# A transformer block on one core: the list of shared items and the work ahead of the first slot are placed anew

## The reference

```python
xn = _layernorm(x)                                   # x: (8, 512, 256)
Q, K, V = xn @ W_q.T, xn @ W_k.T, xn @ W_v.T         # 16 heads of 16
scores = einsum('bhqd,bhkd->bhqk', rope(Q), rope(K)) * 16 ** -0.5
heads  = einsum('bhqk,bhkd->bhqd', softmax(causal(scores)), V)
attn   = heads.reshape(b, t, d) @ W_o.T
ffn    = fake_quant_fp8(xn) @ fake_quant_fp8(weight).T + bias
return x + attn + ffn
```

## Time and profile before

| | us |
|---|---|
| median of the three runs | 439.68 |
| time of the profiled execution | 439.77 |
| its span (first to last instruction) | 438.0 |
| PE, DVE, ACT, POOL busy, share of the span | 88%, 81%, 66%, 56% |
| the chain that ended last, share by engine | PE 63%, ACT 16%, DVE 10%, issue 7%, POOL 2%, DMA 1% |

### The profile page before, as it was taken

One profiled execution on the slowest core, in us unless ns is written; L12 is line 12 of the kernel. 1 busy time (PEld: TensorE's weight loads), 2 busy tenths in 40 slices (PEclk: granted clock), 3 DMA queues, 4 the chain that ended last, 5 costly groups with the idle time before them and its releaser, 6 DMA issues.

```text
span 438.0 us, 9484 instructions
## 1 busy us (share of the span) xinstructions
PE 384.9 (88%) x2990; PEld 205.9 (47%) x2990; DVE 355.3 (81%) x1380; ACT 290.6 (66%) x487; POOL 245.4 (56%) x266
## 2 busy tenths in 40 slices
PE   7998987878879988998899898989899998898886
PEld 7685543333434544454445444545445433353335
DVE  3899679999888988898888979887989797879104
ACT  3529538567765777587866776676677677669751
POOL 5444263365559548556666666676666565245750
PEclk9996979999989999999999999999999999999999
DMA  8944032302503143302630262018031613020111
GB/s 280 307 146 71 1 94 79 73 2 97 123 0 75 52 157 62 75 27 94 148 75 1 98 171 61 15 52 216 15 62 49 183 38 74 2 99 4 49 49 49
DMA packets 27810, 36.40 MB, mean 83 GB/s; under 512 B 3984, under 2 KB 25872, under 8 KB 26320
## 3 DMA queue, kind: packets, MB, share of 16 engines
q1 hardware_dynamic: 27760, 35.79, 30.2%
HBM read 22.94 MB, written 12.58 MB: 81 GB/s over the span
## 4 chain that ended last, share of the span: by engine, by line
PE 63%; ACT 16%; DVE 10%; issue 7%; POOL 2%; DMA 1%; ACTq 0%; POOLq 0%; SPq 0%; DVEq 0%
PE o_ps L1047 15%; ACT prob L803 12%; PE st_ps L943 9%; PE m_ps L927 9%; PE m_ps L1005 7%; PE m_ps L982 7%; PE s_ps L962 5%; DVE scratch L657 4%; PE m_ps L989 2%; PE s_ps L899 2%; DVE prod L605 2%; DMA q_st<-shift 1%; PE m_ps L1013 1%; DVE prod L604 1%; DVE amax L593 1%
## 5 line engine op out<-in xcount | busy, mean ns | idle before, releaser
L803 ACT ACTIVATE prob<-st_ps,exp_scale 128x512 f32<-128x512 f32 x320 | 202.9, 689 | 98.9 <-PE st_ps L943 98.2
L657 DVE CUSTOM_DVE_ANT_0 scratch<-s_ps,causal 128x512 bf16<-128x512 f32 (+3 forms) x512 | 221.3, 484 | 35.8 <-PE s_ps L962 33.8
L510 POOL TENSOR_SCALAR_AFFINE_SELECT prob<-prob 128x512 f32<-128x512 f32 (+1 forms) x160 | 90.1, 565 | 147.4 <-ACT prob L803 147.3
L943 PE MATMUL st_ps<-q_st,k_st 50*128 50x128 f16 (+3 forms) x512 | 108.9, 303 | 35.4 <-ACT prob L803 26.9
L962 PE MATMUL s_ps<-k_st,q_st 48*128 48x512 f16 (+3 forms) x512 | 109.7, 306 | 4.7 <-DVE rowmax L657 4.4
L943 PEld LDWEIGHTS st_ps<-q_st,k_st 50*128 50x128 f16 x512 | 35.2, 94 | 121.1 <-ACT prob L803 74.6
L1047 PE MATMUL o_ps<-prob,v_sb 128*17 128x512 f32 (+3 forms) x1024 | 82.8, 441 | 1.7 <-POOL prob L510 0.9
L962 PEld LDWEIGHTS s_ps<-k_st,q_st 48*128 48x128 f16 x512 | 34.5, 95 | 15.9 <-DVE rowmax L657 9.0
L657 DVE DVE_READ_ACCUMULATOR2_ANT rowmax<- 128x1 f32 x512 | 41.1, 80 | 0.0
L1047 PEld LDWEIGHTS o_ps<-prob,v_sb 128*17 128x17 f32 x1024 | 23.2, 97 | 30.0 <-issue 23.0
L982 PE MATMUL m_ps<-wv_sb,xnT 128*128 128x256 f32 x128 | 33.7, 408 | 1.5 <-ACT v_sb L810 1.3
(11 more groups left out here) (130 smaller groups left out, 493.5 us busy)
## 6 DMA issues: line engine op xcount, KB each, us to landing
qk_parts<-parts SPq DMA_DIRECT2D x14, 512.0 KB, 3.6
xnT<-x_dram SPq DMA_DIRECT2D x8, 512.0 KB, 8.5
q_st<-qk_parts SPq DMA_DIRECT2D x15, 256.0 KB, 4.2
k_st<-qk_parts SPq DMA_DIRECT2D x15, 256.0 KB, 4.6
x_res<-x_dram SPq DMA_DIRECT2D x7, 512.0 KB, 3.4
out_dram<-x_res SPq DMA_DIRECT2D x7, 512.0 KB, 3.0
...
```

The costliest lines, as they stand in the source:

```text
L510: eng.affine_select(out=ap, in_=ap, compare_op=ALU.is_ge, fill=0.0, base=0, pattern=pat, channel_multiplier=-1).then_inc(masked, 1)
L657: eng.tensor_tensor_reduce(scratch[:, at % 3, col:col + w], s_ps[at % 3][:, col:col + w], causal[:, T - w:T], 1.0, NEG, ALU.add, ALU.max, ...
L803: eng.activation(prob[u][:, half * T:(half + 1) * T], st_ps[ST_BANK[2 * s + half]][:, :], ACT.Exp, scale=exp_scale[:, 0:1]).then_inc(exp_d ...
L943: mm = eng.matmul(st_ps[ST_BANK[i]][:, col:col + T - kb * P], k_rows(n, h, ROWS + SHIFT, slice(kb * P, (kb + 1) * P)), q_rows(n, h, ROWS + ...
```

## The change

The tables are written anew. A batch's 20 shared items become 18, since `at` now turns two blocks of queries into one bank, and ACT copies them in one instruction. Four buffers are doubled: `v_sb`, `x_res` and `xq` have one half per parity of the batch, `attnT` has a place for each of the four blocks. Offsets of a batch's items, before and now:

| item | before | now |
|---|---|---|
| v | 0, 2 | -1, 0 |
| mt | -4, 1, 7, 12 | -4, 1, 6, 11 |
| o | 23, 24, 25, 26 | 23, 24, 27, 28 |
| at | 28, 29, 32, 34 | 27, 33 |
| fin | 31, 34, 36, 38 | 29, 34, 42, 45 |
| qk | -32, -30, -27, -25 | -30, -28, -25, -23 |

Batch 1's projections move from slots -7 to -4 to slots -11, -11, -9 and -8 (a slot -11 is added, with no scores in it). `statistics(4, 5)` moves from ahead of the first slot to slot -9 and `statistics(6, 7)` from -9 to -7; `turn_rows` of 2 to 7 moves from -10, -9, -8, -7, -5, -3 to -10, -8, -6, -5, -3, -2; `normalise` has a table of its own. Two stretches of dummy matmuls (16 and 10) with a wait on DMA between them become one of 24.

```diff
-TURN_SLOT = {2: -LEAD, 3: -LEAD + 1, 4: -LEAD + 2, 5: -LEAD + 3, 6: -LEAD + 5, 7: -LEAD + 7}
+STAT_SLOT, INVERT_SLOT = {4: -9, 6: -7}, {4: -8, 6: -6}
+NORMAL_SLOT = {4: -8, 5: -7, 6: -5, 7: -4}
+TURN_SLOT = {2: -10, 3: -8, 4: -6, 5: -5, 6: -3, 7: -2}
...
-CHAIN = {("rotate", 0): -29, ("high", 0): -28, ("low", 0): -26, ("write", 0): -25, ("rotate", 1): -24, ("high", 1): -23,
-         ("low", 1): -21, ("write", 1): -20, ("read", 0, 0): -19, ("read", 0, 1): -16, ("read", 1, 0): -12,
+CHAIN = {("rotate", 0): -27, ("high", 0): -26, ("low", 0): -24, ("write", 0): -22, ("rotate", 1): -22, ("high", 1): -21,
+         ("low", 1): -19, ("write", 1): -17, ("read", 0, 0): -16, ("read", 0, 1): -14, ("read", 1, 0): -8,
...
-    first, last, loop = (24, 25, 26, 27, 28), (6, 7, 11, 12, 14), (16, 17, 21, 22, 24)
+    first, last, loop = (24, 25, 26, 27, 28), (6, 7, 11, 12, 14), (16, 18, 20, 23, 25)
...
-                n = batch_at(slot, -34, 2)
+                n = batch_at(slot, -32, 2)
                 if n is not None:
                     split_x(n)
...
-                n = residual_at(slot, 29, 17)
+                n = residual_at(slot, 27, 17)
...
-                n = batch_at(slot, -35, 2)
+                n = batch_at(slot, -34, 2)
                 if n is not None:
                     high_x(n)
...
                     copy_turned(n)
-                    if n + 2 < NB:
-                        normalise(n + 2)
+                for n in [n for n, at_slot in NORMAL_SLOT.items() if at_slot == slot]:
+                    normalise(n)
...
+            def turn_two(n, i, bank):
+                turn_attn(n, 2 * i, bank, 0)
+                return turn_attn(n, 2 * i + 1, bank, D)
...
             keep_busy(20)
             eng.wait_ge(low_done[1], 2)
-            keep_busy(16)
-            eng.wait_ge(parts_out[1], 16)
-            keep_busy(10)
+            keep_busy(24)
```

135 lines of the change are left out of this document (64 added, 71 removed).

## The result

The changed kernel takes **447.48 us** (median; 446.93 to 448.82 over 4 runs) against 440.38 us for the kernel before in the same call (439.63 to 443.5): ratio 1.0152, 95% interval 1.0095 to 1.0209. It is slower by 1.5%, where 428.5 us was forecast, 2.5% faster.

A forecast was written before the change was run, and what follows sets the result against it. PE nearly full in steady batches (42.17 of 46.2 us), DVE in batch 0. Gains of 7.2 (batches 2 to 5), 1.9 (batch 1), 0.8 (batch 6) and 1.3 (head) sum to 11.2 us: 428.5 us, range 419.0 to 439.0.

The forecast's parts named there:

- Steady batches: Batches 2 to 5: PE's idle time falls from 4.1 to 2.3 us a period; gain 1.8 each, 7.2 us together.
- Wait (1): Slot 28: PE's V product waits for ACT's copy of heads; 1.0 us a batch, bounds 0.6 and 1.3.
- Wait (2): Slots 14 and 19: ACT's `high` waits behind POOL's 2.5 us rotation; 0.7 us for both, bounds 0 and 1.5.
- Wait (3): Slots 3 to 8: POOL's quantisation, bias, split end just in time for slot 10's projection; 0.2 us, bounds 0 and 2.36.
- Batch 1: Batch 1: the steady 1.8 us plus half of 1.3 for half-clock V products, less 0.6 in slot 19; gain 1.9 us.
- scale of two elements: Batch 1's chain on DVE: 2.07 us beside a POOL operation, kept; with a 1.28 us rotation there, batch gain 2.7.
- Batches 6 and 7: Batch 6 gains 0.8 us, its projection slots staying empty; batch 7 wins a little, loses by `qv`, counted at nothing.
- Head: Start to slot 1: slot 1 at 64 to 65 us; gain 1.3 us, bounds -2 and +4.7.
- the fourth rival: Head: PE at 1.2 GHz up to slot 1 costs 3.3 us more, time 431.8; chance 0.1 within the forecast's 0.5.
- Batch 0 at nothing: Batch 0: DVE sets the pace and its work is the same; gain nothing, bounds -1 and +1.
- POOL's queue: Slot 10 of each batch: PE waits 2.36 us for POOL's late `split_x`; time 444.7, chance 0.08.
- The clock: Head: gaps between PE's turns bring half clock up to slot 1, 3.3 us more, time 431.8; chance 0.1.

The follow-up runs named there:

- e10: Changed kernel with the edits of e5, e2, e7 and e8 together, and the last two turns of heads one slot earlier: 435.19 us, ratio 0.9876.
- e12: The kernel of e10 with ACT's `high` copies one slot later and POOL's split of x moved ahead of the bias: 423.88 us, ratio 0.9595.
- e5: Changed kernel with POOL's two quantisation steps of batch 0 in slots 29 and 30, batch 0's first output product in 32: 442.41 us, ratio 0.9994.
- e2: Changed kernel with ACT's three scalings of the weights in slot 20 behind the copy of V's first half: 445.35 us, ratio 1.0117.
- e4: Changed kernel with batch 6's output products back in slots 151, 154, 156 and 158, its store in 159: 445.83 us, ratio 1.0128.
- e8: Changed kernel with ACT's norms of batches 6 and 7 one slot earlier, in slots -6 and -5: 445.65 us, ratio 1.0070.
- e3: Changed kernel with the head of the kernel before put back: 444.15 us, ratio 1.0092.
- e6: Changed kernel with idle PE products added (6, 6, 6 and 16) in slots 156 to 159: 451.14 us, ratio 1.0197.
- e7: Changed kernel with batch 7's bias on POOL in slot 156 in place of 157: 444.76 us, ratio 1.0055.

## Why the prediction was wrong

- **Steady batches: right.** Forecast 44.4, measured 44.23; 7.7 us for 7.2. The terms were less good than their sum, and that their errors cancelled is luck. PE's work fell by 0.6 us that I had not counted; its idle time is 2.6 us for the 2.3 forecast. Wait (1), the copy of heads, is in the trace with 0.73 us of PE, but was not worth its 1.0: in e10 and e12 it is gone and the period is no shorter. Wait (2), `high` behind the rotation, was costed at 0.7 and was 1.5 (bound 1.5). Wait (3), POOL in slots 3 to 8, was costed at 0.2 and showed nothing, but had only 0.2 us of reserve, which the earlier heads used up.
- **Batch 1: wrong in sign,** 10.3 us longer for 1.9 shorter. Two steps failed. I took POOL's slots of a steady batch for all batches and did not lay batch 0's own row of the table (24 to 28) beside the moved bias, split and product; e5 gives 6.0 us back. And I priced the V item in slot 19 against DVE but did not ask what the one in slot 20 waits for: its bank, freed by a copy that ACT's program has behind three scalings; e2 gives 3.5 back. The half clock on slot 26's V products, which I had hoped to halve, stayed (2.67 us for 2.76), and more was added in slots 20, 29 and 30: 0.89 over the batch for 0.97, where I had named 1.00 from batch 1 on as a sign of being right. The chain's scale of two elements, carried over at 2.07 us, took 0.17: POOL ran nothing beside it, so the rotation that I had put there did not stand there either.
- **Batches 6 and 7: undersized,** 4.5 us gained for 0.8. Batch 7's 2.0 us come from a row of the change that neither the table of the change nor the prediction has: batch 6's output products stand in slots 149, 150, 154 and 155, where they stood in 151, 154, 156 and 158. e4 puts them back and the 2.0 us are gone. Where batch 6's 2.5 come from no run asked.
- **Head: wrong in sign,** slot 1 at 69.3 for 64 to 65. The chain that I summed (norm 6, `high`, norm 7, copies, turn, V) is the one in the trace, but started at 54.6 where my sum had 52.0, and ran at half clock, as the fourth rival had it. The start, 2.6 us late, and what the half clock added behind it (V 3.44 us for 1.99, a turn 1.09 for 0.66) make most of the 4.8. The norm of 6 stood behind the copy of batch 5's turn, which I had ending at 52.0 us; the turn ended at 53.6 and its copy at 54.7. I named the chain and left this order as it was: e8 shows that the norm was free from 51.7 on.
- **Batch 0 at nothing: wrong,** 2.0 us, in e3 still 1.7. DVE was busy 0.57 us more and idle 2.04 for 0.64. Of the idle time 0.73 us are its wait for the spread product behind V, which I had costed at 0.6 and booked to batch 1, though it falls in slot 19; 0.81 are a wait for PE's scores at 82.7 us, in a stretch at half clock that the kernel before does not have there (the granted clock over the batch is 0.84 for 0.95). Why DVE was busier, and why other executions of the same slots took up to 45.4 us, is open.
- **Tail at nothing: wrong,** 4.0 us. The prediction had no step for it. Moving batch 6's products forward out of slots 156 to 158 left PE light in front of the tail, and the clock fell (e4, e6); the bias in front of the last masks kept it low for longer (e7). Batch 7 gained by the same move: undoing it brings 1.5 us net (e4).
- **The rivals.** *POOL's queue* was nearest by its number (444.7), by luck: PE did wait for POOL, but in batch 1 alone, through the quantised input and not through slot 10 in every batch. *The clock* came true in the head, where the half clock held from 46.9 to 66 us, with the late norm on top of it. The range was drawn from the errors of the terms that I had. What failed was outside them: the batches whose tables differ from the loop's.
